# Splitting the last 48 inner rows of each routed expert's down product into rounded parts

## The chip, the core and the metric

The kernel runs on one core of one Trainium2 chip, in one launch. The time is the device time of that core, in microseconds (us). Three runs of the kernel before gave a median of 705.6 us (705.32 to 710.57).

## The reference, cut to what matters

The reference is two transformer layers on 1024 tokens of width 256. Each layer adds an attention and a feed-forward part to its input. The change touches only layer 0's feed-forward part, a mixture of 32 routed experts of which every token uses four (up to 128 tokens for each expert), beside one shared expert. For a routed expert `e`:

```
B, S, H = (2, 256, 256)
E, K, F = (32, 4, 176)
CAP = 128
...
w_gate (E, H, F), w_up (E, H, F), w_down (E, F, H)
```

For the tokens `x` of an expert the result is `(silu(x @ w_gate[e]) * (x @ w_up[e])) @ w_down[e]`. The inner width is 176, so the down product sums over a first tile of 128 inner rows and a rest of 48.

## The kernel before, in words

Each engine has an instruction stream of its own, written out by hand in program order; semaphores connect them. The stages follow each other: normalisation, latents and the shared expert (0 to about 88 us), attention of layer 0 together with the routed experts (88 to about 332 us), the combination of the experts' results, and layer 1.

In the attention stage the work is cut into 64 units (8 pairs of heads, 8 units each: `p` is the pair, `u` the unit). Every unit has three places at which work of the experts may be put in. `expert_places` spaces the experts six places apart, so one expert takes two units and a pair of heads holds four experts; the last six are five places apart. What an expert `e` does, with units counted within a pair:

- In an odd unit, TensorE (PE) first makes the unit's scores, then transposes the gathered rows of expert `e` (`rows_turn`, L1873), then the down product of expert `e-1` (`down`, L1888), then the attention's transposes (L1958) and value products (L1967), then in units 1 to 5 a piece of the next pair's projections (L1938, L1927), and last the gate and up products of `e` (`gate_up`, L1881). VectorE (DVE) reduces the scores (L1500), copies out the result of `e-1` (`results_out`, L1442) and then the transposed rows of `e` (`rows_out`, L1436), without which PE may not start L1881.
- In the next, even unit, ScalarE (ACT) takes the tanh of the gates (L1017) and DVE makes the hidden values (`hidden`: L1447, L1449 for the first 128 inner rows, L1450 for the last 48), after its reduction L1500. PE waits for them (`ex_h`) before the row transposes of the following odd unit.
- GpSimd (POOL) stores the result of `e-1` with an indirect DMA (`store`, L818) at place 0 of the odd unit and gathers the rows of `e+2` (`gather`, L812) at the gate products' place. In units 3 and 5 it first waits until all gathers and stores under way have landed (`transfers_landed`) and rotates the next pair's queries with three products (L826, L829, L830); these are ahead of the store in its program.
- SyncE loads the down weights of `e+2` (L715) once the down product of `e` is done.

Both down products are plain f32 matmuls of 128 rows by 256 columns. The rest's tile has 48 rows of values and zeros below. TensorE runs an f32 matmul as two records in the trace; a product of f32r (rounded) operands is one.

## Time and profile before

| what | us |
|---|---|
| median of three runs | 705.6 |
| the profiled execution, its own time | 705.79 |
| its span (first to last instruction) | 704.0 |
| PE busy | 675.8 |
| DVE busy | 489.2 |
| ACT busy | 409.9 |
| POOL busy | 283.6 |

The profiled execution is 0.2 us above the median. The span is 1.8 us shorter than its time. Each busy figure is the union of an engine's instructions, and matmuls overlap each other, so PE's share of 96% doesn't mean that PE is never waiting for an operand. TensorE's granted clock is 1.00 of full speed (2.4 GHz) in every stretch.

### The profile page before, as it was taken

Reading aid. Unit: us, or ns where it says so; the run is one execution under the profiler, and the core shown is the slowest. Engines: PE = TensorE matmul, PEld = TensorE weight load, DVE = VectorE, ACT = ScalarE, POOL = GpSimd, SP = SyncE. Lnnn points to the kernel's source line nnn. Section 1 sums busy time; section 2 is a strip of 40 time slices with the busy share of each in tenths; the row PEclk is TensorE's granted clock in tenths of the full one; section 3 lists DMA queues with packets and bytes.
Section 4 is the critical chain, followed back from the end, with each engine's and each line's share of the span. In section 5 each row is a group of like instructions: output and inputs, shape, how many; then the busy total and the mean of one; then the engine's idle time right before and its main releaser. Section 6 shows DMA issues by size and latency. Waiting matters only on the chain.

```text
span 704.0 us, 13698 instructions
## 1 busy us (share of the span) xinstructions
PE 675.8 (96%) x4708; PEld 576.5 (82%) x4708; DVE 489.2 (69%) x1422; ACT 409.9 (58%) x1069; POOL 283.6 (40%) x289
## 2 busy tenths in 40 slices
PE   6999999999999999998999989999989999999997
PEld 3787888888988888887786655666889999999997
DVE  7898877787778778777784786777465554644544
ACT  3855168788788888888212678888654222222221
POOL 1584144646455464631004308999333410400000
PEclk9999999999999999999999999999999999999999
DMA  8902034453544444351900000200300000000000
GB/s 320 350 0 98 15 123 146 131 187 98 172 132 151 134 142 139 96 162 59 397 15 1 1 1 2 106 1 3 120 1 2 1 1 16 1 16 2 1 16 15
DMA packets 26725, 59.42 MB, mean 84 GB/s; under 512 B 3147, under 2 KB 12749, under 8 KB 26273
## 3 DMA queue, kind: packets, MB, share of 16 engines
q1 hardware_dynamic: 23584, 50.35, 21.1%
q0 software_dynamic: 3072, 8.20, 3.4%
q8 instruction: 38, 0.62, 0.4%
q14 instruction: 31, 0.25, 0.1%
HBM read 48.24 MB, written 10.49 MB: 83 GB/s over the span
## 4 chain that ended last, share of the span: by engine, by line
PE 75%; DVE 14%; ACT 6%; issue 4%; POOL 1%; DMA 0%; DVEq 0%; SPq 0%; ACTq 0%
PE bank L2167 11%; PE bank L1947 7%; PE bank L1881 6%; PE bank L2216 5%; PE bank L1938 5%; PE bank L2190 5%; PE bank L1967 3%; PE bank L1888 3%; PE bank L2078 3%; PE bank L1958 3%; PE bank L2009 3%; PE bank L2230 2%; PE bank L2136 2%; PE bank L2102 2%; ACT sb L1141 2%
## 5 line engine op out<-in xcount | busy, mean ns | idle before, releaser
L1037 ACT ACTIVATE sb<-bank,sb 128x256 f32<-128x256 f32 x128 | 59.6, 471 | 40.6 <-DVE sb L1500 33.1
L1500 DVE TENSOR_REDUCE sb<-bank 128x2 f32<-128x512 f32 x64 | 43.7, 684 | 47.5 <-PE bank L1947 47.1
L1947 PE MATMUL bank<-sb 128*128 128x256 f32 x256 | 66.1, 381 | 0.0
L1206 ACT ACTIVATE h_parts<-sb 128x256 fp32r<-128x256 f32 x56 | 23.4, 418 | 71.3 <-DVE sb L1736 43.4
L1727 DVE TENSOR_TENSOR sb<-sb,bank 128x256 f32<-128x256 f32 x56 | 23.5, 419 | 58.1 <-ACT sb L1170 58.1
L2167 PE MATMUL bank<-rounded,b_hi 128*128 128x256 f32 x224 | 63.1, 282 | 0.0
L2167 PE MATMUL bank<-am_lo,b_hi 128*128 128x256 f32 x224 | 63.0, 281 | 0.0
L2167 PE MATMUL bank<-rounded,b_lo 128*128 128x256 f32 x224 | 63.0, 281 | 0.0
L1170 ACT ACTIVATE sb<-bank 128x256 f32<-128x256 f32 x56 | 21.5, 383 | 62.4 <-PE bank L2167 62.4
L1044 ACT ACTIVATE sb<-sb 128x256 f32<-128x256 f32 x128 | 57.7, 504 | 0.1
L818 POOL DMA_INDIRECT expert_out<-sb x32 | 33.1, 1034 | 60.3 <-DVE sb L1442 44.1
L1141 ACT ACTIVATE sb<-sb 128x128 f32<-128x128 f32 (+1 forms) x128 | 50.6, 445 | 9.8 <-DVE sb L1701 9.0
L1881 PEld LDWEIGHTS bank<-sb 128*128 128x128 f32 (+1 forms) x384 | 46.5, 186 | 5.9 <-DVE sb L1436 4.0
L1881 PE MATMUL bank<-sb 128*128 128x128 f32 (+1 forms) x384 | 48.8, 277 | 1.7 <-DVE sb L1436 1.6
L812 POOL DMA_INDIRECT sb<-rows_x,sb x32 | 32.8, 1026 | 41.4 <-PE bank L1881 16.2
L1947 PEld LDWEIGHTS bank<-sb 128*128 128x128 f32 x256 | 45.2, 190 | 4.8
L1701 DVE CUSTOM_DVE_ANT_1 sb<-bank,sb 128x128 f32<-128x128 f32 (+1 forms) x128 | 38.1, 354 | 14.0 <-ACT sb L1121 9.7
L1967 PE MATMUL bank<-pt_parts,xt_parts 128*128 128x256 f32 x256 | 45.9, 301 | 1.7 <-DVE sb L1517 1.7
L1511 DVE TENSOR_TENSOR pt_parts<-bank,pt_parts 128x512 fp32r<-128x512 f32 x64 | 43.7, 683 | 4.5 <-ACT pt_parts L1057 3.6
L1738 DVE TENSOR_TENSOR h_parts<-sb,h_parts 128x256 fp32r<-128x256 f32 x56 | 25.9, 463 | 27.4 <-ACT h_parts L1206 27.4
L1938 PE MATMUL bank<-rounded 128*128 128x512 f32 x160 | 42.7, 399 | 0.2 <-ACT sb L1066 0.2
L2167 PEld LDWEIGHTS bank<-rounded,b_lo 128*128 128x128 f32 x224 | 42.2, 188 | 0.0
(302 smaller groups left out, 1924.8 us busy)
## 6 DMA issues: line engine op xcount, KB each, us to landing
sb<-in_w_gate_up SPq DMA_DIRECT2D x32, 368.0 KB
sb<-in_w_down SPq DMA_DIRECT2D x32, 256.0 KB
sb<-in_w_pair SPq DMA_DIRECT2D x8, 704.0 KB
expert_out<-sb SPq DMA_DIRECT2D x1, 4096.0 KB, 23.2
sb<-expert_out SPq DMA_DIRECT2D x8, 512.0 KB, 7.4
sb<-in_w SPq DMA_DIRECT2D x1, 1792.0 KB, 15.4
sb<-in_b SPq DMA_DIRECT2D x1, 1792.0 KB, 7.0
sb<-in_sw_up SPq DMA_DIRECT2D x1, 1536.0 KB, 8.8
```

Of the source, the lines that this page charges most:

```text
L1037: act.activation(probs[:, u % 4, q, :], bank[3 + u % 2][:, q * S:(q + 1) * S], ACT.Exp, scale=-1.0, bias=row_min[:, u % 4, q:q + 1], accum ...
L1044: ins = act.activation(probs[:, slot, q, :], probs[:, slot, q, :], ACT.Copy, scale=row_inv[:, slot, q:q + 1])
L1141: act.activation(probs1[:, n % 4, a:b], masked[:, n % 4, a:b], ACT.Exp, scale=-1.0, bias=row_min[:, n % 4, q:q + 1]).then_inc(bl_exp, 1)
L1500: dve.tensor_reduce(row_min[:, u % 4, :], bank[3 + u % 2][:, :].rearrange("p (q n) -> p q n", q=QT), AX.X, ALU.min).then_inc(at_min, 1)
L1511: dve.tensor_tensor(r(probs_lo[:, u % 2]), bank[5 + u % 2][:, :].rearrange("p (a b) -> p a b", a=QT), probs_hi[:, u % 2], ALU.subtract).th ...
L1701: dve.tensor_tensor_reduce(masked[:, n % 4, a:b].rearrange("p (n c) -> p n c", c=CHUNK), bank[SCORE_BANK[n % 4]][:, a:b].rearrange("p (n c ...
L1881: mm = pe.matmul(bank[1][0:n, to:to + P], w_gu[s][:, k, a:a + n], xeT[s][:, k, :], start=(k == 0), stop=(k == KD - 1))
L1938: mm = pe.matmul(where[:, :], r(w[i][:, cols]), r(q[:, half]), start=(n == 0), stop=(n == len(terms) - 1))
L1947: mm = pe.matmul(bank[3 + u % 2][:, q * S:(q + 1) * S], qb[i][:, h, b * S + q * P:b * S + (q + 1) * P], keys[:, h, b * S:(b + 1) * S], sta ...
L1967: mm = pe.matmul(bank[2 + 5 * h][:, 0:S], r(v_parts[:, QT * b + k, :]), r(part[:, u % 2, k, :]), start=(n == 0), stop=(n == len(terms) - 1))
L2167: mm = pe.matmul(dst, lhs, rhs, start=False, stop=(n == len(terms) - 1), skip_group_check=True)
L2190: pe.matmul(dst, r(w[:, 2 * k + j, :]), r(x[:, k, :]), start=(i + j == 0), stop=False, skip_group_check=True)
```

## The change

The 48 rest rows of the hidden values are written three times now: as f32 (`e_hid`), rounded to f32r in rows 0 to 47 of a new tile `e_rest`, and what the rounding left (a `tensor_tensor` subtract on DVE) in its rows 64 to 111. The weight tile of the rest holds its 48 rows twice, at 0 and at 64. ACT rounds it into `w_dn_hi` (`rest_high`), POOL subtracts in place for the low part (`rest_low`). The rest's f32 matmul becomes two f32r matmuls, `e_rest` by `w_dn_hi` and `e_rest` by `w_dn_lo`, which together sum all four products of high and low parts. `e_rest` is zeroed once. The first 128 rows stay f32.

```diff
@@ lay_out
-    out["w_down"] = np.concatenate([f["L0_ffn_w_down"], np.zeros((E0, 2 * P - F0, D), np.float32)],
-                                   1).reshape(E0, 2, P, D).transpose(0, 2, 1, 3)
+    wd = f["L0_ffn_w_down"]
+    gap = np.zeros((E0, UP_AT - FR, D), np.float32)
+    out["w_down"] = np.concatenate([wd, gap, wd[:, P:], gap], 1).reshape(E0, 2, P, D).transpose(0, 2, 1, 3)
...
@@ gpsimd
+            def rest_low(e, s):
+                pool.wait_ge(w_high, SU_STEPS + e + 1)
+                pool.tensor_tensor(r(w_dn_lo[s][:, :]), w_dn[s][:, 1, :], w_dn_hi[:, s, :], ALU.subtract).then_inc(w_low, 1)
...
                         if e:
                             store(e - 1, (e - 1) % SETS)
                             stores += 1
+                        if e is not None and e < E0:
+                            rest_low(e, e % SETS)
...
@@ scalar
+            def rest_high(e, s, before):
+                if e == 0:
+                    act.wait_ge(at_v, 4)
+                act.wait_ge(ed_in[s], 16 * before + 16)
+                act.activation(r(w_dn_hi[:, s, :]), w_dn[s][:, 1, :], ACT.Copy).then_inc(w_high, 1)
+
             def experts(p, u, place):
+                e = EXPERT_COPY.get(place_of_unit(p, u, place))
+                if e is not None and e < E0:
+                    rest_high(e, e % SETS, e // SETS)
...
@@ vector, hidden
-                dve.wait_ge(ex_gu, e + 1)
+                dve.wait_ge(ex_gu, 3 * e + 1)
+                rest_gate, rest_up = e_gu[0:FR, s, 1], bank[1][UP_AT:UP_AT + FR, P:2 * P]
+                dve.scalar_tensor_tensor(e_hid[0:FR, s, 1], rest_gate, 0.5, rest_up, ALU.mult, ALU.mult).then_inc(ex_gu, 1)
+                dve.scalar_tensor_tensor(r(e_rest[0:FR, s]), rest_gate, 0.5, rest_up, ALU.mult, ALU.mult).then_inc(ex_gu, 1)
                 dve.scalar_tensor_tensor(e_hid[:, s, 0], e_gu[:, s, 0], 0.5, bank[1][:, 2 * P:3 * P], ALU.mult, ALU.mult)
-                dve.scalar_tensor_tensor(e_hid[0:FR, s, 1], e_gu[0:FR, s, 1], 0.5, bank[1][UP_AT:UP_AT + FR, P:2 * P],
-                                         ALU.mult, ALU.mult).then_inc(ex_h, 1)
+                dve.wait_ge(ex_gu, 3 * e + 3)
+                dve.tensor_tensor(r(e_rest[LO_AT:LO_AT + FR, s]), e_hid[0:FR, s, 1], e_rest[0:FR, s], ALU.subtract).then_inc(ex_h, 1)
...
@@ vector, before the first unit
                 if i == HALF:
+                    dve.wait_ge(at_v, 3)
+                    dve.memset(e_rest, 0.0).then_inc(at_v, 1)
...
@@ tensor
             def down(e, s, before):
-                pe.wait_ge(ed_in[s], 16 * before + 16)
-                for f in range(2):
-                    mm = pe.matmul(bank[1][:, KD * P:KD * P + D], e_hid[:, s, f, :], w_dn[s][:, f, :],
-                                   start=(f == 0), stop=(f == 1))
-                mm.then_inc(ex_done, 1)
+                dst = bank[1][:, KD * P:KD * P + D]
+                pe.wait_ge(w_low, SU_STEPS + e + 1)
+                pe.matmul(dst, e_hid[:, s, 0, :], w_dn[s][:, 0, :], start=True, stop=False)
+                pe.matmul(dst, r(e_rest[:, s, :]), r(w_dn_hi[:, s, :]), start=False, stop=False)
+                pe.matmul(dst, r(e_rest[:, s, :]), r(w_dn_lo[s][:, :]), start=False, stop=True).then_inc(ex_done, 1)
```

Three places of the changed program in the order of its instructions; a row names the line, the operation, its output and inputs, and the semaphores that it waits on.

POOL, before, units 3 and 5 of a pair (L826 to L830 rotate the queries, L818 is the store, L812 the gather):

```order
L826 TENSOR_TENSOR sb<-sb 128x512 [waits y_stored1,eb_in1,at_qrope,y_stored0,eb_in0]
L829 TENSOR_TENSOR sb<-sb 64x512 [waits at_qe,at_s]
L830 TENSOR_TENSOR sb<-sb 64x512
L818 DMA expert_out<-sb 4096x256 [waits ex_y,at_qe]
L812 DMA sb<-rows_x,sb 128x256 [waits ex_g]
L826 TENSOR_TENSOR sb<-sb 128x512 [waits y_stored1,eb_in1,at_qrope,y_stored0,eb_in0]
```

And in the changed program (L843 to L847 rotate, L831 stores, L836 is `rest_low`, L825 gathers):

```order
L843 TENSOR_TENSOR sb<-sb 128x512 [waits y_stored1,eb_in1,at_qrope,y_stored0,eb_in0]
L846 TENSOR_TENSOR sb<-sb 64x512 [waits at_qe,at_s]
L847 TENSOR_TENSOR sb<-sb 64x512
L831 DMA expert_out<-sb 4096x256 [waits ex_y,at_qe]
L836 TENSOR_TENSOR w_dn_lo<-sb,w_dn_hi 128x256 [waits w_high]
L825 DMA sb<-rows_x,sb 128x256 [waits ex_g]
L843 TENSOR_TENSOR sb<-sb 128x512 [waits y_stored1,eb_in1,at_qrope,y_stored0,eb_in0]
```

`rest_low` stands behind the rotation and the store, and ahead of the gather on which the next rotation's wait for landed transfers depends.

DVE, an even unit from its reduction on, before:

```order
L1500 TENSOR_REDUCE sb<-bank 128x2 [waits at_exp,at_s]
L1506 RECIPROCAL sb<-sb 128x2 [waits at_norm,at_exp]
L1447 SCALAR_TENSOR_TENSOR sb<-sb,bank 128x256 [waits ex_act]
L1449 SCALAR_TENSOR_TENSOR sb<-sb,bank 128x128 [waits ex_gu]
L1450 SCALAR_TENSOR_TENSOR sb<-sb,bank 48x128
L1511 TENSOR_TENSOR pt_parts<-bank,pt_parts 128x512 [waits at_tout]
```

And changed:

```order
L1531 TENSOR_REDUCE sb<-bank 128x2 [waits at_exp,at_s]
L1537 RECIPROCAL sb<-sb 128x2 [waits at_norm,at_exp]
L1475 SCALAR_TENSOR_TENSOR sb<-sb,bank 128x256 [waits ex_act]
L1478 SCALAR_TENSOR_TENSOR sb<-sb,bank 48x128 [waits ex_gu]
L1479 SCALAR_TENSOR_TENSOR e_rest<-sb,bank 48x128
L1480 SCALAR_TENSOR_TENSOR sb<-sb,bank 128x128
L1482 TENSOR_TENSOR e_rest<-sb,e_rest 48x128 [waits ex_gu]
L1542 TENSOR_TENSOR pt_parts<-bank,pt_parts 128x512 [waits at_tout]
```

Two instructions are added ahead of everything else that DVE does in the unit, and PE's `ex_h` comes with the last of them.

PE, the start of an odd unit, before:

```order
L1873 MATMUL bank<-sb 128x128 [waits eb_in0,ex_h]
L1873 MATMUL bank<-sb 128x128
L1888 MATMUL bank<-sb 128x256 [waits ed_in1]
L1888 MATMUL bank<-sb 128x256
L1958 MATMUL bank<-sb 128x128 [waits at_lo,at_norm]
```

And changed:

```order
L1906 MATMUL bank<-sb 128x128 [waits eb_in0,ex_h]
L1906 MATMUL bank<-sb 128x128
L1921 MATMUL bank<-sb 128x256 [waits w_low]
L1922 MATMUL bank<-w_dn_hi,e_rest 128x256
L1923 MATMUL bank<-w_dn_lo,e_rest 128x256
L1991 MATMUL bank<-sb 128x128 [waits at_lo,at_norm]
```

The down product's wait is no longer for the DMA of its weights but for POOL's `rest_low`, and it stands ahead of the f32 matmul as well.

## Rows read from the trace of the kernel before

**Rows 1.** The page's part 1; windows: length, busy PE, PEld, DVE, ACT, POOL.

```profile
PE 675.8 (96%) x4708; PEld 576.5 (82%) x4708; DVE 489.2 (69%) x1422; ACT 409.9 (58%) x1069; POOL 283.6 (40%) x289
...
200.00:250.00 50.00, 49.64 (x329) 44.39 (x328) 38.42 (x104) 41.79 (x119) 26.20 (x27) 1.00 0.49 156
```

**Rows 2.** Chain of waits, units 6 and 7: start us, us, what.

```profile
201.81 0.88 PE bank L1947 x4
...
202.71 0.03 DVE sb L1500
...
203.47 0.33 DVE sb L1447
...
204.12 0.29 DVE sb L1450
...
206.37 0.42 DVE sb L1436
...
206.84 1.59 PE bank L1881 x12
```

**Rows 3.** The same chain, later: down product, transposes, rounded products.

```profile
212.18 0.87 PE bank L1888 x4
213.05 0.44 PE bank L1958 x4
213.49 0.48 PE bank L1967 x4
```

**Rows 4.** Timeline of POOL, units 3 to 6: start us, us, instruction, idle before, releaser.

```profile
190.31 1.10 POOL L826 TENSOR_TENSOR sb<-sb 128x512 f32<-128x512 f32 x1 [0.74 <-DVE sb L1495]
...
194.96 1.05 POOL L818 DMA_INDIRECT expert_out<-sb  x1 [0.80 <-POOL sb L830]
196.32 1.02 POOL L812 DMA_INDIRECT sb<-rows_x,sb  x1 [0.30 <-issue]
199.33 1.08 POOL L826 TENSOR_TENSOR sb<-sb 128x512 f32<-128x512 f32 x1 [1.99 <-DVE sb L1495]
...
203.97 1.05 POOL L818 DMA_INDIRECT expert_out<-sb  x1 [0.80 <-POOL sb L830]
```

**Rows 5.** Timeline of all engines: row copies, gate products, one down product.

```profile
191.02 0.41 DVE L1436 COPY sb<-bank 128x256 f32<-128x256 f32 x1
...
192.00 1.49 PE L1881 MATMUL bank<-sb 128*128 128x128 f32 x12
...
197.68 0.72 DVE L1495 STREAM_SHUFFLE sb<-bank 128x512 f32<-128x512 f32 x1
...
199.28 0.41 DVE L1436 COPY sb<-bank 128x256 f32<-128x256 f32 x1
...
200.32 1.49 PE L1881 MATMUL bank<-sb 128*128 128x128 f32 x12
...
204.74 1.03 PE L1888 MATMUL bank<-sb 128*128 128x256 f32 x4
...
213.79 0.41 DVE L1436 COPY sb<-bank 128x256 f32<-128x256 f32 x1
...
214.66 1.49 PE L1881 MATMUL bank<-sb 128*128 128x128 f32 x12
```

**Rows 6.** Groups by line and shape, last stage: idle and releaser behind the bar.

```profile
L931 POOL TENSOR_TENSOR a_lo<-sb,a_hi 128x256 fp32r<-128x256 f32 x6 | 6.6, 1095 | 22.9 <-ACT a_hi L1162 22.9
...
L931 POOL TENSOR_TENSOR w_lo<-sb,w_hi 128x256 fp32r<-128x256 f32 x4 | 2.9, 735 | 0.0
```

**Rows 7.** Groups of VectorE before the attention stage (60 to 92 us).

```profile
L1388 DVE TENSOR_TENSOR rounded<-bank,rounded 128x128 fp32r<-128x128 f32 x6 | 1.7, 287 | 2.8 <-ACT sb L981 2.7
```

**Rows 8.** The page's part 5: two ScalarE groups.

```profile
L1037 ACT ACTIVATE sb<-bank,sb 128x256 f32<-128x256 f32 x128 | 59.6, 471 | 40.6 <-DVE sb L1500 33.1
...
L1206 ACT ACTIVATE h_parts<-sb 128x256 fp32r<-128x256 f32 x56 | 23.4, 418 | 71.3 <-DVE sb L1736 43.4
```

**Rows 9.** Waits of the row transposes (line L1873): us, times.

```profile
  DVE sb L1450: 5.4, 8
```

More of the change, by code:

```diff
@@ L121 @@
 SU_HI_AT = SETS * (KD * GU + 2 * D)
+LO_AT = UP_AT
+DN_AT = [SETS * KD * GU + 2 * D * s + D for s in range(SETS)]
+KV_TOK_AT = 2 * (2 * 2 * P + 2 * 3 * KVL + 2 * D) + 2 * TOK
+W_SPLITS = SU_STEPS + E0
 TILE_AT = (0, 1, 2, 4, 5, 3, 6, 7)
@@ L326, in program @@
             su_lo = over("su_lo", start[1] + SU_AT, KD * 2 * NF * P)
+            w_dn_lo = []
+            w_dn_lo.append(over("w_dn_lo0", start[2] + DN_AT[0], D))
+            w_dn_lo.append(over("w_dn_lo1", start[2] + DN_AT[1], D))
             su_hi = over("su_hi", start[2] + SU_HI_AT, KD * 2 * NF * P)
+            w_dn_hi = over("w_dn_hi", start[3] + KV_TOK_AT, SETS * D)
+            e_rest = over("e_rest", start[3] + KV_TOK_AT + SETS * D, SETS * P)
         with ExitStack() as overlay:
@@ L437, in program @@
         w_dn = [r3.take(2, D) for _ in range(SETS)]
+        w_dn_hi = w_dn_hi[:, :].rearrange("p (s n) -> p s n", s=SETS)
+        e_rest = e_rest[:, :].rearrange("p (s n) -> p s n", s=SETS)
         xe = r3.take(SETS, D)
@@ L455, in program @@
         keys = r4.take(2, TOK)
+        assert r4.at == KV_TOK_AT
         kv_tok = r4.take(NT, 3 * KVL)
@@ L587, in program @@
             sem(n) for n in ("at_s", "at_min", "at_exp", "at_inv", "at_norm", "at_t", "at_tout", "at_pv", "at_ctx"))
-        su_high, su_low, x2_lo = sem("su_high"), sem("su_low"), sem("x2_lo")
+        w_high, w_low, x2_lo = sem("w_high"), sem("w_low"), sem("x2_lo")
         at_v, at_lo, at_cl = sem("at_v"), sem("at_lo"), sem("at_cl")
@@ L791, in _ @@
             for n in range(SU_STEPS):
-                pool.wait_ge(su_high, n + 1)
-                pool.tensor_tensor(r(su_step(su_lo, n)), su_step(sw_up, n), su_step(su_hi, n), ALU.subtract).then_inc(su_low, 1)
+                pool.wait_ge(w_high, n + 1)
+                pool.tensor_tensor(r(su_step(su_lo, n)), su_step(sw_up, n), su_step(su_hi, n), ALU.subtract).then_inc(w_low, 1)
             for u in range(2 * NF):
@@ L970, in _ @@
                     act.wait_ge(shared_in, 48)
-                    act.activation(r(su_step(su_hi, i - 3)), su_step(sw_up, i - 3), ACT.Copy).then_inc(su_high, 1)
+                    act.activation(r(su_step(su_hi, i - 3)), su_step(sw_up, i - 3), ACT.Copy).then_inc(w_high, 1)
             act.wait_ge(lat_vr, 1)
@@ L1464, in experts @@
                     if e == 0:
-                        dve.wait_ge(at_v, 1)
+                        dve.wait_ge(at_v, 4)
                     hidden(e, e % SETS)
@@ L1840, in shared_up @@
                         if n == 2 * KD:
-                            pe.wait_ge(su_low, f // 2 + 1)
+                            pe.wait_ge(w_low, f // 2 + 1)
                         mm = pe.matmul(bank[2 * (u % 2) + j][:, :], r(w[:, k, tile]), r(x[:, k, cols]),
```

## The prediction

> **What bounds the kernel now.** I read the page's engine totals first, then the busy time by stretch, the chain of waits through the attention stage, and the timelines around the lines that the change touches. Units are counted within a pair.
>
> PE is busy 96% of the span, and 49.64 of 50 us in a stretch of the attention stage, DVE 38.42, ACT 41.79, POOL 26.20 [rows 1]. That looks like a stage in which only PE's work counts. The chain of waits shows the exception, once in every pair of heads: PE's scores of unit 6 (201.81) hand over to DVE at 202.71, and from there the chain stays on DVE, through the hidden values (203.47 to 204.41) and the row copy (206.37), until PE's gate products start at 206.84 [rows 2]. So from unit 6 to unit 7, where PE has no projection to do, DVE is the bound and has no slack. In the other odd units PE is the bound, and DVE's row copy ends ahead of the gate products by 0.46 us (unit 1: 214.66 - 214.20), 0.57 (unit 3: 192.00 - 191.43) and 0.63 (unit 5: 200.32 - 199.69) [rows 5]; 0.05 of that is the hand-over seen at 206.79 to 206.84 [rows 2], which leaves 0.41, 0.52 and 0.58.
>
> **The change on PE.** The down product takes 0.87 us for two f32 matmuls, 0.435 each; four rounded matmuls of the same width take 0.48, 0.12 each [rows 3]. New: 0.435 + 2 x 0.12 = 0.675, a saving of 0.195 us for each expert, 6.2 us over 32, if PE alone counts.
>
> **The change on DVE.** The 48-row product (0.29 [rows 2]) is done twice, at a pace of 0.30. The subtraction has no row of its own: the nearest rounding subtraction has 128 columns too and takes 287 ns [rows 7]; a free cost (0) and a whole 0.42 copy [rows 2] are the ends, I take 0.28. Together the hidden values are ready 0.58 us later, and all that DVE does behind them is 0.58 later. The cover, unit by unit: unit 1 lacks 0.58 - 0.41 = 0.17, unit 3 0.06, unit 5 nothing: 0.23 us a pair in place of PE's gain, since PE's shorter down product only makes it arrive earlier at the same copy. From unit 6 to 7 all of 0.58 is on the path.
>
> **The change on ACT.** A 128x256 rounding copy takes 418 ns [rows 8]. ACT idles 40.6 us in front of its exponentials, 33.1 of it for DVE's minimum [rows 8]; 32 x 0.42 = 13.4 us fits into that. Cost 0 up to the last pair. Should that cover be gone, 0.42 for each expert shows. Its wait for the weights' DMA is new. Those weights are asked for two units or some 7 us ahead, I take 0.
>
> **The change on POOL, the largest term.** A 128x256 rounding subtraction takes 735 ns, or 1095 in the dearer group [rows 6]. PE needs it before the down product, and it stands behind the rotation and the store. The down product of unit 7 needs the `rest_low` issued in unit 5. Before: rotation of unit 3 at 190.31, store 194.96, gather 196.32, rotation of unit 5 at 199.33, store 203.97, while PE's down product starts at 204.74 [rows 4, 5]. The store of unit 5 is thus already 0.77 us ahead of PE only, and takes 1.05. What the rotation at 199.33 waited for is the gather: DVE had released it at 198.40 [rows 5], 0.93 us earlier, and the distance of 3.01 us from the gather's start repeats in all pairs but one. Now:
>
> - rotation of unit 3, released by DVE: 190.31 + 0.58 = 190.89
> - store 4.65 later, 195.54, with 1.05: 196.59
> - `rest_low` with 0.10 to start and 0.74: 197.43
> - gather with the gap 0.30 [rows 4]: 197.73
> - landed 3.01 later: 200.74, rotation
> - store 4.64 later, 205.38, end 206.43
> - `rest_low` for unit 7: 206.53 to 207.27, hand-over 0.07: PE at 207.34, in place of 204.74.
>
> PE waits 2.60 us there. It then has 0.675 down, 0.44 and 0.48 [rows 3]: 208.94 for the gate products in place of 206.84. So **2.1 us a pair**, in which the 0.58 of DVE is contained (DVE's copies, released by the down product at 208.0, end at 208.8). Ends: 0.58, if POOL is no bound after all; and 2.1 + 0.5 (the gap ahead of the gather as in 0.80 [rows 4]) + 2 x 0.36 (1095 ns each) + 2 x 0.2 (0.30 instead of 0.10 to start) = 3.7. I take 2.1, from the row of the shape itself. POOL catches up behind: the rotation of the next unit 3 starts with DVE again, so nothing accumulates. In units 1, 3 and 5 `rest_low` is in time (unit 5: 196.69 to 197.43, PE about 197.4, a tie).
>
> **Sum.** Six pairs at 2.1: 12.6. The seventh, whose unit 6 belongs to the closer experts: the wait 2.60 less 0.2, 2.4. Units 1, 3, 5: 7 x 0.23 = 1.6. First experts: 0.58 at the first wait for hidden values, plus 0.3 for zeroing 128x256 on DVE (a copy of that size takes 0.42 [rows 2], 0 if another engine is the bound there): 0.9. In the last pair PE has no projections and waits for L1450; 8 such waits are in the whole stage [rows 9], five of them there: 5 x (0.58 - 0.2) = 1.9, and ACT's copy is on the path about twice, 0.8. Total 12.6 + 2.4 + 1.6 + 0.9 + 2.7 = 20.2 us. On the profiled time of 705.8 that is 726.0, and 725.8 on the median. I say **726 us**, 2.9% slower.
>
> **A rule weighed.** POOL's subtraction has one cheap and one dear group, 735 and 1095 ns at the same shape [rows 6]; in the attention stage DVE read no two SBUF operands at once, so I took the cheap one. The Trainium skill (SBUF — State Buffer, Who interferes with whom) says that a DVE instruction with two SBUF inputs and a GpSimd instruction that reads SBUF lock each other out of a shared port, the later one waiting in full. The new DVE subtraction is such an instruction. By that rule the 0.28 or up to 0.74 us would be added where the two meet, at most 7 x 0.74 = 5 us more, 731; this trace has no such pair in this stage. The sum stays.
>
> **The rivals.**
>
> - *DVE alone (chance 0.13).* POOL's program runs further ahead than the gather's landing makes me think, and PE never waits for `rest_low`. Against it: the store's start only 0.77 us ahead of PE, with 1.79 us of work to come. Then 7 x (0.58 + 0.23) = 5.7, + 0.9 + 2.7 = 9.3: 715 us.
> - *POOL worse (0.12).* The dear bounds: 3.7 in six pairs, 4.0 in the seventh, the rest 5.2: 31 us, 737. For it: the one pair with a later landing, and the new meeting of DVE and POOL.
> - *Faster (0.05), the other side.* The saving of PE shows and the rest hides: 705.8 - 6.2 = 699.6. It decides at one point: `rest_low` must end, and the hidden values be ready, before PE asks at 204.74. The chain through DVE in [rows 2] speaks against it, since there not one added instruction is covered.
> - *No change (0.08).* PE's gain in units 1 to 5 (24 x 0.195 = 4.7) is kept because DVE's slack is larger than the copy's end shows, and the waits of unit 7 are nearer to DVE's 0.58: 705.8 - 4.7 + 4.1 + 3.6 = 709.
> - *The rounded matmuls aren't cheap here.* If the two cost 0.435 each, PE's down product becomes 0.87 + 0.435 and the tail and unit 7 pay 0.63 more for each of twelve experts, 7.6: 734. It stands inside the upper part of my range; its chance is in the 0.62 of my forecast.
>
> **Numbers.** Forecast 0.62: 726. The range 714 to 735 takes in the forecast with its own ends and most of the DVE rival. A change of 1% (7 us) is about what a measurement of this kernel can tell from none. Below 698.7: 0.03, since the faster case by itself gives 0.9% and only half of it lies beyond. Within 1%: 0.12, from the rest of it, the no-change case and the lower edge of the DVE rival. Above: 0.85.
>
> **What the profile after would show.** Right: seven waits of PE's down product for POOL's subtraction, each near 2.6 us; the gather 1.4 us later against DVE than before; L1482 near 0.28; 32 subtractions of 735 ns; the down product 0.2 us shorter; ACT's idle time for DVE smaller by some 13 us. Wrong: if PE waits for POOL less than 1 us a pair, the landing of the gather didn't carry the delay on; if ACT's exponentials start late behind its wait for weights, I missed the DMA; if the gate products of units 1 and 3 move by more than 0.3 us, DVE's slack was misread.

## The result and the profile after

The changed kernel takes 736.08 us (median of 6 runs, 733.89 to 736.95), the kernel before 708.05 in the same comparison (6 runs, 705.32 to 711.03): 1.0389 times as long, 95% interval 1.0357 to 1.0421. The forecast was 726 with 714 to 735. The profiled execution after took 735.72, its span 733.9; before 705.79 and 704.0. So 29.9 us are to be accounted for, of which the forecast had 20.2. Up to the last row transposes of the attention stage (321.5 us before, 349.4 after) it is 27.9; the other 2.0 come behind the stage, where the clock of the profiled execution after falls twice more (360 to 368 and 556 to 564 us) and that of before doesn't.

The runs of the kernel before don't lie around one value: of 19 runs in one comparison, five with a mean granted clock of 1.000 (the profiled execution is of this kind) took 705.44 to 705.77 us, four with 0.995 took 707.65 to 707.93, and ten with 0.993 took 709.48 to 710.61, so that below differences to 705.5 are taken only for runs with a clock of 1.000.

The page's part 1, then the stretch of [rows 1] (length; busy PE, PEld, DVE, ACT, POOL; granted clock; DMA share; GB/s):

```profile
PE 688.1 (94%) x4708; PEld 583.9 (80%) x4708; DVE 506.3 (69%) x1487; ACT 419.2 (57%) x1101; POOL 308.1 (42%) x321
```

```profile
200.00:250.00 50.00, 47.70 (x298) 41.70 (x296) 38.38 (x104) 39.65 (x112) 30.39 (x35) 0.97 0.39 117
```

PE's busy time fell from 49.64 to 47.70 us in this stretch, and the shorter down products alone don't explain it: PE waits now, as the next rows show. The clock of 0.97 is new.

What PE's weight loads wait for in the attention stage (line waited for: us in total, times, longest):

```profile
PEld bank L1906 <- DVE e_rest L1482: 12.6, 12, 1.6
PEld bank L1921 <- POOL w_dn_lo L836: 12.0, 7, 2.3
...
PEld bank L1971 <- ACT sb L1094: 2.5, 7, 0.5
```

The first line answers to [rows 9] (the row transposes wait for the hidden values' last part), the second is the wait that the forecast put into unit 7: seven times, as foreseen. The third was in no step of mine. The idle time of ACT in front of its exponentials grew from 40.6 [rows 8] to 48.6, and the part of it for DVE, which I expected to shrink by some 13 us, from 33.1 to 43.9:

```profile
L1065 ACT ACTIVATE sb<-bank,sb 128x256 f32<-128x256 f32 x128 | 59.6, 470 | 48.6 <-DVE sb L1531 43.9
```

The same place as in [rows 2 to 4], units 5 to 7 of a pair, now on POOL's timeline (start, us, instruction, idle before and its releaser). L847 ends the rotation, L831 stores, L836 is `rest_low`, L825 gathers:

```profile
207.79 1.04 POOL L831 DMA_INDIRECT expert_out<-sb  x1 [0.80 <-POOL sb L847]
208.87 0.78 POOL L836 TENSOR_TENSOR w_dn_lo<-sb,w_dn_hi 128x256 fp32r<-128x256 f32 x1
209.80 1.03 POOL L825 DMA_INDIRECT sb<-rows_x,sb  x1 [0.16 <-issue]
212.84 1.08 POOL L843 TENSOR_TENSOR sb<-sb 128x512 f32<-128x512 f32 x1 [2.01 <-issue]
...
217.48 1.04 POOL L831 DMA_INDIRECT expert_out<-sb  x1 [0.80 <-POOL sb L847]
218.56 0.73 POOL L836 TENSOR_TENSOR w_dn_lo<-sb,w_dn_hi 128x256 fp32r<-128x256 f32 x1
219.45 1.02 POOL L825 DMA_INDIRECT sb<-rows_x,sb  x1 [0.16 <-issue]
```

And PE there; L1906 are the row transposes, L1921 to L1923 the down product, L1991 and L2000 the transposes and rounded products, L1914 the gate products:

```profile
217.59 0.44 PE L1906 MATMUL bank<-sb 128*128 128x128 f32 x2 [0.55 <-DVE e_rest L1482]
219.34 1.22 PE L1921 MATMUL bank<-sb 128*128 128x256 f32 x2 [1.32 <-POOL w_dn_lo L836]
220.00 0.78 PE L1922 MATMUL bank<-w_dn_hi,e_rest 128*128 128x256 f32 x1
220.58 0.41 PE L1923 MATMUL bank<-w_dn_lo,e_rest 128*128 128x256 f32 x1
220.79 1.05 PE L1991 MATMUL bank<-sb 128*128 128x128 f32 x4
221.50 1.20 PE L2000 MATMUL bank<-pt_parts,xt_parts 128*128 128x256 f32 x4
222.50 1.60 PE L1914 MATMUL bank<-sb 128*128 128x128 f32 x12
```

The chain runs as forecast: the rotation at 212.84 starts 3.04 us after the gather's start at 209.80, the store is 4.64 later, `rest_low` behind it, and PE 0.05 us behind that. Then comes what I didn't foresee. From 219.34 to 222.50 everything on PE takes about twice as long: the first f32 matmul's record 1.22 for two (0.60 in a quiet unit, below), the transposes 1.05, the rounded products 1.20. The granted clock tells why (the same columns as above):

```profile
212.00:216.00 4.00, 4.00 (x29) 3.67 (x28) 2.38 (x8) 3.94 (x11) 2.94 (x3) 1.00 0.39 97
216.00:220.00 4.00, 2.14 (x10) 1.35 (x9) 3.13 (x10) 3.93 (x13) 3.01 (x4) 0.91 0.27 101
220.00:224.00 4.00, 4.00 (x25) 3.91 (x24) 1.77 (x4) 2.02 (x6) 2.19 (x3) 0.66 0.42 114
```

In 216 to 220 PE was busy 2.14 us of 4, and in the next stretch the clock is 0.66, part of the time at the lower of its two levels, 1.2 instead of 2.4 GHz. The Trainium skill (TensorE: Matmul & The Clock Gate, HAM oscillation — how this bites in real kernels) describes the pattern: a wait that comes once in every round of a loop lets the clock drop, and each next round begins slow. The trace agrees: such a fall (down to 0.61 to 0.71 in the lowest stretch of 4 us) stands in six of the seven pairs, always behind the wait of unit 7. In the pair without one, unit 7 to unit 1 takes 8.52 us, in the first pair 10.69, in four more 9.88 to 9.95; before, 7.33. In the seventh it is 9.70, before 6.02.

The pair without a fall had the same wait: 1.33 us of idle time ahead of its down product at 253.87, where the pair above has 1.32, and PE was busy for 2.12 of the 4 us from 250.5, for 2.14 above. So the length of the wait doesn't decide alone whether the clock falls; what else does, these traces don't show.

That pair (its row transposes of units 1, 3, 5 and 7 at 227.47, 235.65, 244.47 and 252.10) lets me compare the rest with my steps. Distances between the row transposes of successive odd units, us:

| units | before | after, no fall | difference |
|---|---|---|---|
| 1 to 3 | 7.98 | 8.18 | 0.20 |
| 3 to 5 | 8.32 | 8.82 | 0.50 |
| 5 to 7 | 7.30 | 7.63 | 0.33 |
| 7 to 1 | 7.33 | 8.52 | 1.19 |
| pair | 30.93 | 33.15 | 2.22 |

The forecast had 2.1 + 0.23 = 2.33 a pair. Its 2.1 are the chain on POOL from the rotation of unit 3 to the gate products of unit 7, and have to be compared with the last three distances together: 2.02. None of the chain's steps waits for PE in unit 5: in the second to the sixth pair they are 6.64 to 6.66 us from the rotation to the gather, 3.00 to 3.08 to the next rotation and 6.50 to 6.52 to the down product. In these pairs the rotation of unit 3 starts 1.98 to 2.23 us behind that unit's row transposes (1.44 to 1.53 before), and the down product of unit 7 starts 18.21 to 18.41 behind them (15.89 before), that is 2.3 to 2.5 later, for 2.60. So the 0.50 that PE loses between units 3 and 5 is not added to the chain: it stands inside the chain's time, and PE then waits that much less in unit 7. Without the clock's fall, the pair is what the forecast had.

### The profile page after: what moved, and what is told of

Its sections match the earlier page's. It is cut to its first block, busy times and chain, and to the rows that moved or that the text cites. A ratio compares the mean times of both kernels' runs of the same rounds, so it can differ in the third digit from the quotient of the medians.

```text
span 733.9 us, 13828 instructions
## 1 busy us (share of the span) xinstructions
PE 688.1 (94%) x4708; PEld 583.9 (80%) x4708; DVE 506.3 (69%) x1487; ACT 419.2 (57%) x1101; POOL 308.1 (42%) x321
## 4 chain that ended last, share of the span: by engine, by line
PE 41%; DVE 7%; ACT 6%; issue 3%; POOL 1%; DVEq 0%; ACTq 0%; POOLq 0%
PE bank L2200 11%; PE bank L2223 5%; PE bank L2249 5%; PE bank L2111 3%; PE bank L2263 2%; PE bank L2169 2%; PE bank L2135 2%; PE bank L2153 2%; PE bank L2180 2%; ACT sb L1169 2%; DVE sb L1637 2%; PE bank L2279 1%; PE bank L2093 1%; PE bank L2272 1%; ACT sb L1175 1%
## 5 line engine op out<-in xcount | busy, mean ns | idle before, releaser
L1065 ACT ACTIVATE sb<-bank,sb 128x256 f32<-128x256 f32 x128 | 59.6, 470 | 48.6 <-DVE sb L1531 43.9
L831 POOL DMA_INDIRECT expert_out<-sb x32 | 33.0, 1030 | 70.1 <-DVE sb L1470 58.9
L1914 PEld LDWEIGHTS bank<-sb 128*128 128x128 f32 (+1 forms) x384 | 49.3, 199 | 8.5 <-DVE sb L1464 7.6
L1914 PE MATMUL bank<-sb 128*128 128x128 f32 (+1 forms) x384 | 53.1, 291 | 1.9 <-DVE sb L1464 1.0
L2000 PE MATMUL bank<-pt_parts,xt_parts 128*128 128x256 f32 x256 | 49.0, 316 | 1.2 <-DVE sb L1548 1.2
L825 POOL DMA_INDIRECT sb<-rows_x,sb x32 | 33.1, 1036 | 29.1 <-DVE sb L1461 14.8
L1991 PE MATMUL bank<-sb 128*128 128x128 f32 x256 | 40.5, 283 | 2.5 <-DVE pt_parts L1542 2.5
## 6 DMA issues: line engine op xcount, KB each, us to landing
sb<-in_w_pair SPq DMA_DIRECT2D x8, 704.0 KB
```

The source lines that it names most:

```text
L1065: act.activation(probs[:, u % 4, q, :], bank[3 + u % 2][:, q * S:(q + 1) * S], ACT.Exp, scale=-1.0, bias=row_min[:, u % 4, q:q + 1], accum ...
L1914: mm = pe.matmul(bank[1][0:n, to:to + P], w_gu[s][:, k, a:a + n], xeT[s][:, k, :], start=(k == 0), stop=(k == KD - 1))
L1991: mm = pe.transpose(dst[:, k, q * P:(q + 1) * P], probs[:, u % 4, q, k * P:(k + 1) * P], ident)
L2000: mm = pe.matmul(bank[2 + 5 * h][:, 0:S], r(v_parts[:, QT * b + k, :]), r(part[:, u % 2, k, :]), start=(n == 0), stop=(n == len(terms) - 1))
```

## Experiments

Twelve more kernels were run. In the table, the ratio is to the kernel before in the same comparison, and "pair" is the usual distance between the row transposes of the same unit in successive pairs.

| run | us | ratio, 95% interval | pair |
|---|---|---|---|
| before | 705.6 to 709.9 | | 30.9 |
| after | 736.08 | 1.0389, 1.0357 to 1.0421 | 34.6 |
| e1_low_early | 717.54 | 1.0130, 1.0082 to 1.0179 | 32.1 |
| e2_no_low | 717.85 | 1.0117, 1.0072 to 1.0162 | 32.0 |
| e3_one_product | 732.28 | 1.0317, 1.0265 to 1.0370 | 33.4 to 36.1 |
| e4_fill | 731.40 | 1.0324, 1.0280 to 1.0367 | 33.1 to 33.9 |
| e5_early_one_product | 704.78 | 0.9953, 0.9931 to 0.9975 | 30.3 |
| e6_pe_only | 702.71 | 0.9928, 0.9905 to 0.9951 | 30.2 |
| e7_early_small_copy | 716.07 | 1.0121, 1.0078 to 1.0163 | 32.0 |
| e8_wait_late | 724.92 | 1.0245, 1.0191 to 1.0298 | 32.6 |
| e9_early_turn | 717.64 | 1.0135, 1.0098 to 1.0171 | 32.0 |
| e10_where_slack | 710.00 | 1.0026, 1.0008 to 1.0045 | 31.0 |
| e11_dve_only | 718.36 | 1.0151, 1.0118 to 1.0183 | 32.1 |
| e12_two_of_four | 711.13 | 1.0053, 1.0033 to 1.0074 | 31.2 |

**e1_low_early** moves the subtraction in units 3 and 5 ahead of the rotation and its wait for landed transfers.

```diff
@@ gpsimd, units 3 and 5
+                        rest_low(e, e % SETS)
                         transfers_landed(gathers, stores)
...
-                            rest_low(e, e % SETS)
```

> The changed kernel with one move: in units 3 and 5 POOL's subtraction for the weights (rest_low) stands ahead of the wait for landed transfers and the query rotation, instead of behind the store. Everything else is as in the changed kernel. Theory A (POOL's program order makes PE's down product wait in unit 7, and the clock's fall behind that wait is part of its price): PE's waits for POOL in unit 7 go from 1.3-2.3 us to 0, what stays there is DVE's 0.58 us, the granted clock stays 1.00 through the stage, and the time falls from 736 to 715-720. Theory B (DVE's two added instructions and the shorter slack behind them cost nearly all of it, and POOL's wait only fills time in which DVE would be waited for): 731-736.

Measured: 717.54 us, 18.5 below after. The place of one instruction of 0.74 us in POOL's program is the largest part of the loss. In the trace PE's wait for POOL in unit 7 is gone, and the clock is 1.00 through the seven pairs.

**e2_no_low** leaves POOL's subtractions out; the low product reads the high weights again, so the weights' low parts don't enter the result.

```diff
-                pe.wait_ge(w_low, SU_STEPS + e + 1)
+                pe.wait_ge(w_high, SU_STEPS + e + 1)
...
-                pe.matmul(dst, r(e_rest[:, s, :]), r(w_dn_lo[s][:, :]), ...)
+                pe.matmul(dst, r(e_rest[:, s, :]), r(w_dn_hi[:, s, :]), ...)
```

> The changed kernel without POOL's 32 subtractions: the low weight part is left out, the third matmul of the down product reads the high part again, and PE waits for ACT's rounding copy only. Theory A: as fast as the kernel with the subtraction moved, within 2 us (715-719), since POOL's 32 x 0.74 us matter only by where they stand. If POOL's load itself counts, this one is faster than that one by 3 us or more. Theory B: 730-736.

Measured: 717.85, the same as e1 within the spread of the runs (four each). The one run with a clock of 1.000 took 715.58, e1's two took 716.69 and 716.84. So with the early place, POOL's 32 subtractions cost about 1 us at most; what they cost in the change is their place.

**e3_one_product** leaves out DVE's two added instructions in the changed kernel; the hidden values' low part is zero.

```diff
-                dve.scalar_tensor_tensor(e_hid[0:FR, s, 1], rest_gate, 0.5, rest_up, ...)
...
-                dve.tensor_tensor(r(e_rest[LO_AT:LO_AT + FR, s]), e_hid[0:FR, s, 1], e_rest[0:FR, s], ALU.subtract)
```

> The changed kernel without DVE's two added instructions: the 48 rest rows are written once, rounded, and the low part of the hidden values is left out (zeros). POOL, ACT and PE do all that they do in the changed kernel. Theory A: POOL's wait in unit 7 stays (its chain starts 0.58 us earlier, the wait is then 1.0-1.8 us), the clock still falls in some pairs, and the time is 724-729. Theory B: 707-713.

Measured: 732.28 (one of its four runs took 3772.69 us, the other three 730.99 to 732.90, their median 731.66), only some 4 below after, and above what was expected. PE waits for POOL longer instead:

```profile
PE bank L1919 <- POOL w_dn_lo L836: 19.0, 8, 3.8
```

19.0 us in eight waits, where after has 10.4 in seven. POOL's chain sets when unit 7 goes on, and in four of the seven pairs it became longer: the rotation of unit 5 starts 3.59 to 4.64 us behind the gather's start, where the same pairs of after have 3.00 to 3.08. Why the transfers landed later isn't shown. And the clock falls deeper (in after, the two halves of this stretch have 1.00 and 0.61):

```profile
112.00:120.00 8.00, 5.67 (x24) 5.49 (x25) 2.56 (x7) 3.99 (x12) 4.55 (x5) 0.60 0.27 83
```

In the two pairs with an early landing (2.98 and 3.02), the down product of unit 7 comes 17.48 us behind unit 3's row transposes (18.25 and 18.59 in after), so there DVE's saving does shorten the chain. That e3 gains so little is thus the later landing and the deeper fall, as far as the trace shows, and not only one cause hiding behind the other.

**e4_fill** keeps the change and fills a part of PE's wait in unit 7 with three plain matmuls whose result isn't used.

```diff
+                    if u == 7 and p + 1 < PAIRS:
+                        pe.wait_ge(at_qm, 2 * p + 4)
+                        for _n in range(3):
+                            pe.matmul(bank[0][:, 0:D], ident, keys[:, 0, 0:D], start=True, stop=True)
```

> The changed kernel with 21 unused f32 matmuls of 128x256 added: three in each unit 7 of the first seven pairs, 1.3 us, between PE's wait for the hidden values and its row transposes and down product, into a bank that nobody reads then. They fill the time in which PE would wait for POOL. Theory A with the clock's fall as a part of the price (about 1.1 us in each of six pairs): the granted clock stays at 1.00 in more pairs, and the kernel with more work is faster than the changed one by 3-7 us, 729-733. If the fall has nothing to do with PE's idle time: 736 or more, and the clock as before.

Measured: 731.40, 4.7 below after although PE does more. Around two of the seven waits of unit 7:

```profile
112.00:120.00 8.00, 6.74 (x45) 5.89 (x46) 4.66 (x12) 5.20 (x15) 5.75 (x7) 1.00 0.36 99
240.00:256.00 16.00, 14.64 (x99) 12.81 (x97) 10.84 (x30) 12.59 (x37) 9.23 (x9) 1.00 0.42 120
```

The clock stays at 1.00 through the seven pairs, and unit 7 to unit 1 takes 8.47 to 8.56 us in four pairs, as in the undisturbed pair of after (8.52). The wait for POOL is still there, so the clock was a cost of its own. After has 9.88 to 9.95 in four pairs, 10.69 in the first (9.22 here) and 9.70 in the seventh (8.24 here): 1.3 to 1.5 us each, six times, some 8 us. The seven distances from unit 7 to unit 1 are together 10.4 us longer here than in e1, and 7.9 longer in after than here. (The fifth pair has 9.21 here and 8.52 in after: its gather landed later, with the clock at 1.00.) The whole time fell by less, 6.2 us between the profiled executions, because behind the stage the clock of this one falls for longer, from 352 to 368.

**e5_early_one_product** is e1 and e3 together.

```diff
+                        rest_low(e, e % SETS)
                         transfers_landed(gathers, stores)
...
-                dve.scalar_tensor_tensor(e_hid[0:FR, s, 1], rest_gate, 0.5, rest_up, ...)
...
-                dve.tensor_tensor(r(e_rest[LO_AT:LO_AT + FR, s]), e_hid[0:FR, s, 1], e_rest[0:FR, s], ALU.subtract)
```

> The kernel with POOL's subtraction moved ahead (717.5 us) and also without DVE's two added instructions (the low part of the hidden values is left out). Theory C (what is left over the kernel before is DVE's 0.58 us in unit 7 and in the last pair, and some 0.36 us a pair that PE waits for ACT's merged queries behind the new rounding copy): 706-709. Theory D (the rounded matmuls or something else on PE costs time): 712 or more.

Measured: 704.78, 12.8 below e1: with POOL out of the way, DVE's two instructions cost in full (a pair takes 30.3 in place of 32.1). It is below the expected 706 to 709. The hidden values' low part is zero here, so this is no replacement.

**e6_pe_only** keeps of the change only what PE does: ACT rounds only the first two experts' weights, POOL subtracts nothing, DVE makes one product, and the low product reads the high weights. Most weights are stale, so its output isn't the reference's.

```diff
-                if e is not None and e < E0:
+                if e is not None and e < SETS:
                     rest_high(e, e % SETS, e // SETS)
```

> PE's side alone: the down product as in the changed kernel (one f32 and two rounded matmuls, both on the high weight tile), but the weights are split for the first two experts only (30 rounding copies and all subtractions left out) and the hidden rest is written once, rounded. DVE and POOL have the work of the kernel before. Theory C with my price of the rounded matmuls (0.195 us for each expert where PE is the bound, none in unit 7): 3-5 us faster than the fast runs of before, 701-704. Theory D: 706 or more.

Measured: 702.71. The four distances are 7.11, 7.21, 7.79 and 8.13, so 0.19, 0.12, 0.19 and 0.19 shorter: PE's saving of 0.195 is there as forecast, in three of the four places in full. The down product and the transposes behind it:

```profile
209.03 0.60 PE L1918 MATMUL bank<-sb 128*128 128x256 f32 x2
209.28 0.47 PE L1919 MATMUL bank<-w_dn_hi,e_rest 128*128 128x256 f32 x1
209.58 0.28 PE L1920 MATMUL bank<-w_dn_hi,e_rest 128*128 128x256 f32 x1
209.70 0.60 PE L1988 MATMUL bank<-sb 128*128 128x128 f32 x4
```

209.03 to 209.70 is 0.67 us (0.675 forecast, 0.87 before [rows 3]).

**e7_early_small_copy** is e1 with ACT's rounding cut to 8 of 256 columns from the third expert on; most of the weights' high part is stale.

```diff
-                act.activation(r(w_dn_hi[:, s, :]), w_dn[s][:, 1, :], ACT.Copy)
+                n = D if e < SETS else 8
+                act.activation(r(w_dn_hi[:, s, 0:n]), w_dn[s][:, 1, 0:n], ACT.Copy)
```

> The kernel with POOL's subtraction moved ahead (717.5 us), where ACT's rounding copy covers 8 of 256 columns from the third expert on (the other high parts are stale, so the output is not the reference's). Theory C: PE's wait for ACT's merged queries (0.36 us in each of seven pairs) goes, and a little in the last pair: 713-715. If ACT's load is hidden as I predicted: 717-718.

Measured: 716.07, 1.5 below e1, between both expectations and with an interval that overlaps e1's. Units 3 to 5 take 8.78 to 9.04 us where e1 has 8.79 to 9.09, the last pair 0.2 less. ACT's copies are at most a small part; how small isn't settled.

**e8_wait_late** lets the changed kernel's down product wait piece by piece.

```diff
-                pe.wait_ge(w_low, SU_STEPS + e + 1)
+                pe.wait_ge(ed_in[s], 16 * before + 16)
                 pe.matmul(dst, e_hid[:, s, 0, :], w_dn[s][:, 0, :], start=True, stop=False)
+                pe.wait_ge(w_high, SU_STEPS + e + 1)
                 pe.matmul(dst, r(e_rest[:, s, :]), r(w_dn_hi[:, s, :]), start=False, stop=False)
+                pe.wait_ge(w_low, SU_STEPS + e + 1)
```

> The changed kernel (736 us), where PE waits for POOL's low part only before the third matmul of the down product, for ACT's high part before the second, and for the weights' DMA before the first. Theory A: 0.43 + 0.12 us of the product runs inside the wait of unit 7, 0.5 us in each of seven pairs, and with a shorter idle time of PE the clock's fall is rarer: 726-732. If only the total order of POOL counts and the clock falls all the same: 732-734.

Measured: 724.92, 11.2 below after and below the expected range. Unit 7 to 1 takes 7.93 to 8.05 us. GpSimd is as late as before; but PE does 0.55 us of its work ahead of the wait, and the clock stays at 1.00 through the seven pairs, which the expectation had given too little.

**e9_early_turn** is e1 with the hidden values' low part signalled by itself: the row transposes no longer wait for it, only the down product's second matmul does.

```diff
-                dve.scalar_tensor_tensor(e_hid[:, s, 0], ...)
+                dve.scalar_tensor_tensor(e_hid[:, s, 0], ...).then_inc(ex_h, 1)
...
+                pe.wait_ge(x2_lo, 4 + e + 1)
                 pe.matmul(dst, r(e_rest[:, s, :]), r(w_dn_hi[:, s, :]), start=False, stop=False)
```

> The version with the weights' subtraction ahead of the rotation, in which in addition the row transposes of the next expert wait only for the hidden values' first 128 rows, and the subtraction of the rest behind them is waited for only by the second matmul of the down product. Theory A (the subtraction costs as load on VectorE: its later copies are late by it whoever waits for it): no change against that version's 717.5 us, 716.5 to 718.5. Theory B (it costs as latency between VectorE and the row transposes, 0.28 us in each unit 6 and in five units of the last pair, 12 x 0.28 = 3.4): 713 to 715.

Measured: 717.64, no change against e1. Units 5 to 7 become 0.3 shorter (7.34) and 7 to 1 0.3 longer (7.65): the transposes start earlier, and PE then waits for the row copy (11.6 us in all, 10.4 in e1). The subtraction costs as load on DVE, not as latency to PE.

**e11_dve_only** adds two 48x128 products to the kernel before and nothing else.

```diff
+                for spare in (e_hid, e_gu):
+                    dve.scalar_tensor_tensor(spare[UP_AT:UP_AT + FR, s, 1], e_gu[0:FR, s, 1], 0.5,
+                                             bank[1][UP_AT:UP_AT + FR, P:2 * P], ALU.mult, ALU.mult)
```

> The kernel before, with two more 48x128 products on VectorE ahead of the hidden values of every expert, into rows that count for nothing; PE, ScalarE and GpSimd do what they did before. Theory A (VectorE's two added instructions cost more than the uncovered part of the row copies, because the copy's delay goes on through the tanh and the merged queries to the projections between units 3 and 5, and in the last pair): about what the step from one to three products cost with the early subtraction, 12.8 us, less what TensorE's shorter down product gives back, so 714 to 719 us. Rival (what the prediction had for VectorE alone: 5.7 + 0.6 + 1.9 = 8.2, with no shorter down product to be later than): 712 to 714 us.

Measured: 718.36; its one run with a clock of 1.000 took 716.62, which is 11.1 over the 705.5 of before. e1's runs with 1.000 took 716.69 and 716.84. So DVE's load by itself costs as much as the whole change with the early subtraction. PE's saving, seen in e6, shows in e1 only from unit 5 to 7 (7.63 where e11 has 7.82), and as much is lost between 3 and 5 (8.79 to 9.09 for 8.77). The distances are 7.82, 7.33, 8.19 and 8.77, so 0.52, 0, 0.21 and 0.45 more. My 0.58 and 0.17 are near the first and third. The last should have been 0.06. ACT's timeline in unit 3, before (row transposes at 157.92), shows the path that I missed; L1037 are the exponentials, L1017 the tanh, L1065 and L1066 copy the merged queries, for which PE's projections L1938 wait:

```profile
159.79 0.47 ACT L1037 ACTIVATE sb<-bank,sb 128x256 f32<-128x256 f32 x1 [1.04 <-DVE sb L1500]
...
160.70 0.90 ACT L1044 ACTIVATE sb<-sb 128x256 f32<-128x256 f32 x2
161.62 0.38 ACT L1051 ACTIVATE sb<-bank 64x256 f32<-64x256 f32 x1
162.03 0.60 ACT L1057 ACTIVATE pt_parts<-bank 128x512 fp32r<-128x512 f32 x1
162.60 0.38 ACT L1017 ACTIVATE sb<-bank 128x256 f32<-128x256 f32 x1
162.88 0.58 ACT L1065 ACTIVATE sb<-bank 64x512 f32<-64x512 f32 x1
163.47 0.59 ACT L1066 ACTIVATE sb<-bank 64x512 f32<-64x512 f32 x1
```

PE's projections start at 164.17, 0.11 us behind the last row's end at 164.06. From 159.79 on ACT has no gap of more than 0.1 us, in the rows left out neither. The stretch starts when DVE's reduction is ready ("1.04 <-DVE sb L1500"). With two more products, the same unit in e11 (row transposes at 161.00):

```profile
163.40 0.48 ACT L1037 ACTIVATE sb<-bank,sb 128x256 f32<-128x256 f32 x1 [1.56 <-DVE sb L1503]
...
166.13 0.38 ACT L1017 ACTIVATE sb<-bank 128x256 f32<-128x256 f32 x1
166.40 0.59 ACT L1065 ACTIVATE sb<-bank 64x512 f32<-64x512 f32 x1
167.00 0.59 ACT L1066 ACTIVATE sb<-bank 64x512 f32<-64x512 f32 x1
```

```profile
164.15 1.59 PE L1884 MATMUL bank<-sb 128*128 128x128 f32 x12
...
167.64 1.43 PE L1941 MATMUL bank<-rounded 128*128 128x512 f32 x5
```

The exponentials start 2.40 us behind the row transposes in place of 1.87, the merged queries end at 167.59, and the projections start 6.64 behind the transposes in place of 6.25. The gate products at 164.15 are 3.15 behind the transposes, the same as before (130.13 behind 126.98 in the second pair): there my slack held. The cover that I read at the row copy was not the one that was used up.

**e10_where_slack** computes all, and splits only those of the first 26 experts whose down product isn't in unit 7. ACT rounds the hidden rest, DVE's subtraction is a place later, the weights' subtraction early, the waits piece by piece. The core:

```diff
+SPLIT = [e for e in range(E0 - 6) if e % 4 != 2]
...
+                if e not in RANK:
+                    pe.matmul(dst, e_hid[:, s, 1, :], w_dn[s][:, 1, :], start=False, stop=True).then_inc(ex_done, 1)
+                    return
```

> The whole computation, with the split kept for those 20 experts of the first 26 whose down product isn't in unit 7; the others keep the f32 matmul. The rounding of the hidden rest is done by ScalarE, VectorE's subtraction comes one place later, the weights' subtraction stands ahead of the rotation in unit 3, and the down product's waits stand each ahead of the matmul that needs them. Theory A (what the change costs is on VectorE and GpSimd in front of units 7 and in the last pair, and TensorE's saving of 0.195 us for each expert is real elsewhere): 20 x 0.195 = 3.9 us faster than before at best, less what VectorE's subtraction takes of the cover in units 1 to 5: 701 to 706 us. Rival (VectorE has no slack in units 1 to 5 either, so 20 subtractions of 0.28 us show in full and the saving doesn't): 708 to 712 us.

Measured: 710.00, not faster. Units 5 to 7 and 7 to 1 take 7.10 and 7.21 (0.20 and 0.12 less than before), but 3 to 5 takes 8.60 to 8.84 in place of 8.32. All 12 runs have a clock of 0.990 to 0.998; with 0.995, four runs of before took 707.89 to 708.18 and a fifth 709.69, seven of these 708.88 to 710.83.

**e12_two_of_four** goes further: no added work in units 4 and 6.

```diff
-SPLIT = [e for e in range(E0 - 6) if e % 4 != 2]
+SPLIT = [e for e in range(E0 - 6) if e % 4 in (0, 3)]
```

> The whole computation, with the split only for those two of each four experts (of the first 26) whose down product is in unit 1 or 3, so that none of the added work of GpSimd is in front of the rotations of units 3 and 5, and none of VectorE's in units 4 and 6. The other down products are as before. Theory A (the added work has cover in units 0 and 2, and none in 4 and 6): unit 7 to 1 7.20, 1 to 3 8.01, 3 to 5 8.13, 5 to 7 7.30 us, 30.64 a pair in place of 30.93, so 1.7 to 2 us faster than before: 703 to 705 us. Rival (each subtraction shows wherever it stands): 707 to 709 us.

Measured: 711.13, slower, and above the rival's 709 as well. The runs with a clock of 0.995 took 710.31 to 711.36, those of before in this comparison 707.65 to 707.80, so the clock doesn't explain the 3 us. In the trace the last row transposes of the stage come 2.4 us later than before. Units 3 to 5 still take 8.59 to 8.81, with nothing added in unit 4. DVE's timeline from the end of unit 2 into unit 3 says why (L1491 is the subtraction, L1536 and L1538 belong to the next queries' rotation, L1543 is the reduction that ACT waits for, L1469 the row copy):

```profile
127.66 0.29 DVE L1491 TENSOR_TENSOR e_rest<-sb,e_rest 48x128 fp32r<-48x128 f32 x1
127.97 0.69 DVE L1536 TENSOR_TENSOR sb<-bank,sb 128x512 f32<-128x512 f32 x1
...
128.59 0.73 DVE L1538 STREAM_SHUFFLE sb<-bank 128x512 f32<-128x512 f32 x1
129.22 0.68 DVE L1543 TENSOR_REDUCE sb<-bank 128x2 f32<-128x512 f32 x1
...
129.88 0.41 DVE L1475 COPY sb<-bank 128x256 f32<-128x256 f32 x1
130.20 0.42 DVE L1469 COPY sb<-bank 128x256 f32<-128x256 f32 x1
```

There is no gap from the subtraction to the row copy, nor ahead of it back to unit 2's reduction at 124.98. DVE is full from there on, so what is added in unit 2 delays the reduction of unit 3 in full: ACT's exponentials, which waited 1.18 us for it, start 2.22 us behind the row transposes (at 127.71) in place of 1.87. What is left is unit 0, with cover for one expert in four: at most 7 x 0.195 = 1.4 us; that wasn't run.

## Why the prediction was wrong

- **PE's saving, 0.195 us each: right.** 0.67 for the down product (e6).
- **POOL's subtraction, 735 ns: right.** 32 instructions of 723 to 827 ns, median 739. DVE's subtraction has a median of 285 (0.28 forecast), ACT's copy 409 (418):

```profile
L836 POOL TENSOR_TENSOR w_dn_lo<-sb,w_dn_hi x32: 723/739/827, 91.3 to 353.5; 128x256 fp32r<-128x256 f32 x32
```

```profile
L1482 DVE TENSOR_TENSOR e_rest<-sb,e_rest x32: 284/285/712, 96.5 to 355.8; 48x128 fp32r<-48x128 f32 x32
```

- **POOL's chain, the largest term: right, nearly in size too.** Seven waits, where forecast. Behind unit 3's row transposes the down product of unit 7 came 2.3 to 2.5 us later, for 2.60, and in the pair without a fall the next unit 1 came 2.02 later, for 2.1. What was off are small steps: the gap ahead of the gather, 0.16 in place of 0.30, and the two behind the stores, 0.04 in place of 0.10. PE's weight loads waited 12.0 us in seven (1.7 each, not 2.6), since PE came to the wait late itself by what it had lost since unit 3. In e4, without a fall, the seven distances from unit 3 to the next unit 1 are together 16.7 longer than before, where the sum had 12.6 + 2.4 = 15.0. Of this, e1 against after gives 18.5 us less the clock's 8, so about 10.5, as the price of the chain over what DVE costs anyway.
- **The step that failed: the clock.** "PE waits 2.60 us there. It then has 0.675 down, 0.44 and 0.48" prices the work behind the wait at the durations before it. At half the clock it took 3.16 us from 219.34 to 222.50, in place of 1.595 (1.78 in the pair without a fall), and in each of six pairs the way to the next unit 1 is 1.3 to 1.5 us longer than in e4, where the clock doesn't fall: some 8 us that stand in no term, no bound and no rival. Without them it would have been about 728, inside the range.
- **A second step that was mis-sized: DVE's cover.** "The cover, unit by unit: unit 1 lacks 0.58 - 0.41 = 0.17, unit 3 0.06, unit 5 nothing" looked at one consumer of DVE, the row copy. Another one, the reduction that starts ACT's exponentials, tanh and merged queries, had 0.11 us in unit 3. There 0.45 us shows (e11) in place of 0.06. The case "DVE alone", priced at 9.3 us net, costs 11.1 (e11), and as much with all of the change but POOL's order (e1). In the changed kernel itself this step cost little: the 0.45 lies inside POOL's chain, which binds from unit 3 to unit 7. That the sum of a pair came out so near (2.22 for 2.33) was in part luck, since the forecast didn't know of this overlap.
- **The sum, by the runs:** 10.5 (chain) + 8 (clock) + 11.2 (the rest, e1) = 29.7 of 29.9. It is no check of its own, since the 18.5 and the 11.2 are steps of the same ladder; what the traces add is the split of the 18.5.
- **ACT, cost 0:** not refuted (e7). But its idle time for DVE grew by 10.8 us instead of shrinking by 13: here an engine that waits for a late engine got its new work for nearly nothing and idled more.
- **The rule weighed, up to 5 us: right where it applies.** Of 32 subtractions of DVE, five are longer than 0.29 us: 0.71 at 96.48, 0.54 at 268.03, 0.43 at 200.25, 0.42 at 112.49 and 0.34 at 165.65. All five start while POOL is in an instruction that reads SBUF, a rounding copy or subtraction or a product of the rotation. The longest:

```profile
96.18 0.86 POOL L822 TENSOR_TENSOR rounded<-sb,rounded 128x128 fp32r<-128x128 f32 x2
```

```profile
96.48 0.71 DVE L1482 TENSOR_TENSOR e_rest<-sb,e_rest 48x128 fp32r<-48x128 f32 x1
```

DVE's instruction starts within POOL's (96.18 to 97.04) and ends 0.15 us behind it. The Trainium skill (SBUF — State Buffer, Who interferes with whom) names just this: a VectorE instruction with two SBUF inputs contends with a GpSimd instruction that reads SBUF. The trace agrees, with 0.43, 0.25 and three times 0.05 to 0.15 us, 1.0 in all in place of the up to 5 that I weighed. Where DVE was first, in seven places, POOL's `rest_low` behind it took 0.75 to 0.83 us in place of 0.74, less than the rest of DVE's instruction; and at 268.03 POOL's instruction had 0.40 us left, of which DVE's became 0.25 longer. That the later one waits in full, as I weighed it, is not seen.
- **The rivals.** "POOL worse", 737, has the time but not the cause: none of its dear bounds came. "Faster" asked for what e6 shows to be there, a gain of PE (701.08 for 705.79 us between the profiled executions), and for cover that wasn't.

## What to carry to other kernels

A wait of PE in a busy stage costs more than its length: when the trace of before shows a clock of 1.00 throughout, price the work behind a new wait (here idle times of 1.3 to 2.0 us) at both levels of the clock, and keep both. A short instruction costs what stands behind it in its engine's program, so put it ahead of a wait, not behind (18.5 us by the place of 0.74 us). And the slack of an engine is the smallest over all who wait for it, read by following each hand-over to the next consumer of PE; where its timeline has no gap over two units, there is none.
